# A four-layer conditional chain on one core: which engine casts x, and when the mixing matrices are made

## The reference

```
layers 0 and 2 (mix):  h   = gelu(gelu(cond @ W0 + b0) @ W1 + b1)
                       att = softmax(h @ W2 + b2)                  # 8 weights per example
                       out = (sum_k att[k] * weight[k]) @ x + att @ bias_k
layers 1 and 3 (conv): out = conv1d(x, weight, 9 taps, pad 4, 4 groups)
                             + cond @ c_weight.T + side
```

## Time and profile before

| | us |
|---|---|
| median of 3 runs | 2923.36 (2922.13 to 2923.71) |
| the profiled execution | 2924.14 |
| its span, first to last instruction | 2922.3 |
| TensorE busy | 2888.9 (99%) |
| VectorE busy | 2396.4 (82%) |
| ScalarE busy | 1394.9 (48%) |
| GpSimd busy | 1411.1 (48%) |
| mean granted TensorE clock | 0.992 of full |

### The profile page before, as it was taken

One profiled execution on the slowest core, in us unless ns is written; L12 is line 12 of the kernel. 1 busy time (PEld: TensorE's weight loads), 2 busy tenths in 40 slices (PEclk: granted clock), 3 DMA queues, 4 the chain that ended last, 5 costly groups with the idle time before them and its releaser, 6 DMA issues.

```text
span 2922.3 us, 123031 instructions
## 1 busy us (share of the span) xinstructions
PE 2888.9 (99%) x49220; PEld 2878.5 (99%) x49220; DVE 2396.4 (82%) x3099; ACT 1394.9 (48%) x2077; POOL 1411.1 (48%) x1545
## 2 busy tenths in 40 slices
PE   6999999999999999999999999999999999999998
PEld 5999999999999999999999999999999999999998
DVE  7888888878888887888888888878888888888884
ACT  3545454444445454544444454544444444545444
POOL 3454444545454444445454545445454545444442
PEclk7999999999999999999999999999999999999999
DMA  4777777777777777777777777777777777777774
GB/s 136 187 195 203 199 202 201 198 201 201 201 195 201 200 200 199 202 199 198 200 201 201 196 203 202 195 200 202 202 196 202 198 201 197 204 203 194 200 203 135
DMA packets 375112, 573.69 MB, mean 196 GB/s; under 512 B 63400, under 2 KB 227376, under 8 KB 358704
## 3 DMA queue, kind: packets, MB, share of 16 engines
q1 hardware_dynamic: 326320, 506.70, 64.8%
q10 hardware_dynamic: 48768, 66.65, 9.2%
HBM read 272.15 MB, written 167.77 MB: 151 GB/s over the span
## 4 chain that ended last, share of the span: by engine, by line
PE 97%; DVE 1%; DMA 1%; ACT 0%; ACTq 0%; SPq 0%; issue 0%; DVEq 0%
PE ps L309 73%; PE ps L294 24%; DMA x_t<-x 1%; ACT x_t L455 0%; DVE prod L528 0%; DVE xp L494 0%; DVE m_sum L532 0%; ACTq L471 0%; DVE m_own L536 0%; DVE y L563 0%; ACT y L430 0%; SPq L178 0%; DVE conv_raw L502 0%; DVE att_table L515 0%; DMA mixed<-m_own 0%
## 5 line engine op out<-in xcount | busy, mean ns | idle before, releaser
L309 PE MATMUL ps<-y,conv_parts 32*128 32x512 f32 x36864 | 2590.2, 390 | 2.2 <-DVE y L563 2.2
L309 PEld LDWEIGHTS ps<-y,conv_parts 32*128 32x128 f32 x36864 | 2469.9, 183 | 7.3 <-issue 3.3
L563 DVE SCALAR_TENSOR_TENSOR y<-ps,bias,y 128x512 fp32r<-128x512 f32 x1536 | 1066.9, 746 | 450.5 <-ACT y L430 443.8
L430 ACT ACTIVATE y<-ps,bias 128x512 fp32r<-128x512 f32 x1536 | 1047.0, 690 | 763.3 <-PE ps L309 718.0
L632 POOL TENSOR_TENSOR xp<-x_t,xp 128x512 fp32r<-128x512 f32 x512 | 709.9, 1417 | 564.3 <-DVE xp L494 564.3
L458 ACT ACTIVATE o_ph<-ps,bias 128x512 f32<-128x512 f32 x508 | 327.8, 687 | 736.4 <-PE ps L309 733.5
L639 POOL COPY o_t<-o_ch 128x512 f32<-128x512 f32 x508 | 636.0, 1373 | 9.7 <-DMA o_ch<-o_ph 9.7
L294 PE MATMUL ps<-y,m_parts 32*128 32x512 f32 x6144 | 582.2, 391 | 7.4 <-DVE y L563 7.4
L294 PE MATMUL ps<-xp,m_parts 32*128 32x512 f32 x6144 | 585.2, 391 | 0.8 <-issue 0.5
L626 POOL COPY bias<-bias_table 128x4 f32 (+3 forms) x512 | 94.8, 201 | 928.0 <-DMA o_ch<-o_ph 881.4
L294 PEld LDWEIGHTS ps<-y,m_parts 32*128 32x128 f32 x6144 | 524.9, 183 | 8.1 <-issue 7.8
(11 more groups left out here) (40 smaller groups left out, 43.4 us busy)
## 6 DMA issues: line engine op xcount, KB each, us to landing
x_t<-x SPq DMA_DIRECT2D x512, 256.0 KB, 5.3
m_parts<-mixed SPq DMA_DIRECT2D x1024, 128.0 KB, 5.2
out<-o_t SPq DMA_DIRECT2D x127, 1024.0 KB, 3.9
o_ch<-o_ph SPq DMA_DIRECT2D x1016, 64.0 KB, 2.0
o_ch<-o_ph ACTq DMA_DIRECT2D x1016, 64.0 KB, 2.1
mixed<-m_own SPq DMA_DIRECT2D x256, 128.0 KB, 2.4
conv_raw<-conv_w SPq DMA_DIRECT2D x2, 768.0 KB, 11.2
mix_sb<-mix_w SPq DMA_DIRECT2D x2, 576.0 KB, 11.2
```

What stands on the lines that cost most here:

```text
L309: ins = nc.tensor.matmul(ps[:, 4 + t, :], conv_parts[layer][rows, w, PH * q + p_in, :], src[rows, a, p_in, q:q + N], start=(k == 0), stop= ...
L430: nc.scalar.activation(dst, src, ACT.Identity, bias=bias[layer][:, k % WIDTH[layer]:k % WIDTH[layer] + 1]).then_inc(high_set[layer], 1)
L563: nc.vector.scalar_tensor_tensor(out=dst, in0=src, scalar=bias[layer][:, k % WIDTH[layer]:k % WIDTH[layer] + 1], in1=high.bitcast(fp32), o ...
```

## The change

VectorE's program before the steps puts `att_rows(0)` and matrix (0, 0) directly behind the softmax. `x_high` moves from VectorE to ScalarE: `x_high(0)` behind ScalarE's `att_rows(0)`, and in the steps behind the high parts of layer 0. The identity of conv 1 comes behind matrix (0, 0) and the `att_t` copies. Matrix (0, 1) is made ahead of the low part of conv 1's taps. The matrix of layer 2 is made one step later: matrix (2, i) in step i instead of matrix (2, i + 1). SP's transfers follow: x of example 1 is loaded in step -1 directly behind matrix (0, 0), and the store of matrix (2, i) stands behind the shuffle DMAs.

```diff
--- before.py
+++ after.py
@@ -215,18 +215,22 @@
                 if has(i, inner, 3):
                     sp.wait_ge(in_time_set, 4 * (i - 2))
                     sp.dma_start(out[i - 3], o_t[:]).then_inc(out_done, 16)
+                if not inner and i == -1:
+                    sp.wait_ge(x_low_set, 4)
+                    load_x(1)
+                if not inner and i == 0:
+                    store_matrix(2, 0)
+                    load_matrix(2, 0, True)
                 if has(i, inner, -2):
                     store_matrix(0, i + 2)
-                if has(i, inner, -1):
-                    store_matrix(2, i + 1)
-                if not inner and i == -1:
-                    load_matrix(2, 0, True)
                 if has(i, inner, 2) and (inner or not is_last(i)):
                     for g in range(G // 2):
                         sp.wait_ge(phases_set, nth(i - 2, g))
                         for p in range(PH):
                             sp.dma_start(o_ch[CG * g:CG * (g + 1), p, :], o_ph[CG * p:CG * (p + 1), g, :]).then_inc(shuffled[p], 16)
-                if has(i, inner, -2):
+                if has(i, inner, 0) and (inner or i != 0):
+                    store_matrix(2, i)
+                if has(i, inner, -2) and (inner or i != -1):
                     sp.wait_ge(x_low_set, 4 * (i + 2))
                     load_x(i + 2)
                 if not inner and is_last(i):
@@ -407,7 +411,16 @@
                 nc.scalar.copy(att_table[:, :, l, 0:4].rearrange("c j k -> c k j"),
                                ps[:, 6 - 2 * l, :].rearrange("c (k j) -> c k j", k=4)).then_inc(table_act, 1)
 
+            def x_high(j, first):
+
+                act.wait_ge(x_in, 16 * G * (j + 1))
+                if not first:
+                    act.wait_ge(mm[0], 4 * j)
+                for g in range(G):
+                    nc.scalar.copy(xp[:, HIGH, g, :], x_t[:, g, :]).then_inc(x_high_set, 1)
+
             att_rows(0)
+            x_high(0, True)
             conv_high_part(1)
             att_rows(1)
             for l in range(2):
@@ -438,6 +451,8 @@
                 if now:
                     for q in range(G):
                         high(0, i, q, segment(HIGH, q), by_phase(q), not inner and i == 0)
+                if now and has(i, inner, -1):
+                    x_high(i + 1, False)
                 if before:
                     final = not inner and is_last(i)
                     for g in range(G):
@@ -485,14 +500,6 @@
                 ins.then_inc(dve_chain, 1)
                 dve.wait_ge(dve_chain, chained[0])
 
-            def x_high(j, first):
-
-                dve.wait_ge(x_in, 16 * G * (j + 1))
-                if not first:
-                    dve.wait_ge(mm[0], 4 * j)
-                for g in range(G):
-                    nc.vector.tensor_copy(xp[:, HIGH, g, :], x_t[:, g, :]).then_inc(x_high_set, 1)
-
             def conv_identity(layer):
 
                 dve.wait_ge(conv_in[layer], 16)
@@ -548,15 +555,16 @@
                 dve.wait_ge(expo_set, l + 1)
                 chain(nc.vector.reciprocal(inv[:, l:l + 1], total[:, l:l + 1]))
                 nc.vector.tensor_scalar(att_sb[:, l, :], expo[:, l, :], inv[:, l:l + 1], None, ALU.mult).then_inc(att_set, 1)
-            x_high(0, True)
-            conv_identity(1)
             att_rows(0)
             matrix(0, 0, True)
             for l in range(2):
                 dve.wait_ge(att_t_mm, l + 1)
                 nc.vector.tensor_copy(att_t[:, l, :], ps[0:K, l, 0:B]).then_inc(att_t_set, 1)
+            conv_identity(1)
             att_rows(1)
+            matrix(0, 1, False)
             conv_low_part(1)
+
             def low(layer, j, k, dst, src, high):
 
                 dve.wait_ge(high_set[layer], nth(j, k))
@@ -572,13 +580,11 @@
                     for q in range(G):
                         low(0, i, q, segment(LOW, q), by_phase(q), segment(HIGH, q))
                 if not inner and i == 0:
-                    x_high(i + 1, False)
-                if has(i, inner, -2):
+                    matrix(2, 0, True)
+                if now and has(i, inner, -2):
                     matrix(0, i + 2, False)
-                if has(i, inner, -1):
-                    matrix(2, i + 1, not inner and i == -1)
-                if now and has(i, inner, -1) and (inner or i != 0):
-                    x_high(i + 1, False)
+                if now and (inner or i != 0):
+                    matrix(2, i, False)
                 if not inner and is_last(i):
                     dve.wait_ge(bias_set[3], B)
                     dve.wait_ge(x_low_set, 4 * B)
```

## The result

The changed kernel takes 2910.51 us (median of 6 runs, 2907.53 to 2912.03), the kernel before 2923.33 on the same chip (2922.13 to 2923.71): 12.8 us less, ratio 0.9955 [0.9945, 0.9966] (in brackets here and below: the 95% interval of the ratio). The sign and the mechanism came as written, but the forecast gain is 3.5 us too small. The profiled execution took 2910.93 with a span of 2908.7 (before 2922.3), at a mean clock of 0.995.

What follows compares the result with a forecast made beforehand. TensorE, 99% busy, was taken to bound the kernel, winnable only in its waits before the loop is full. Example 2 9.3 us earlier (9.0 + 2.2 - 1.9), loop 0: from 2923.36 to 2914.0 us, range 2910.8 to 2919.

Steps and rivals of the forecast that it cites:

- Which wait bounds the kernel: Before the loop is full: TensorE's 7.42 us wait ahead of layer 2 of example 0, on VectorE, delayed by late x.
- Part 1, matrix (0, 0): At the start: first matrix ends at 20.2, held by GpSimd (bounds 18.2 and 20.5), so layer 0 starts 2.0 us earlier.
- Part 2, the clock: From layer 0 of example 0 to example 1: of 2.0 us gained, 1.1 arrives, by when the clock rises; example 1 at 47.0.
- Part 3, layer 2: Layer 2 of example 0 starts at 52.1, not 61.11: 9.0 us gained, bounds 51 and 53.7.
- Part 3, the clock in the dip: From layer 2 of example 0 to example 2: the clock no longer falls, 2.2 us gained (bounds 0 and 2.2).
- Part 3, VectorE late at example 2: Layer 0 of example 2 waits for bank 0, freed late by VectorE: 1.9 us lost (bounds 0 and 3.7).
- Part 4, the loop: In the full loop: ScalarE's added casts and VectorE's held matrices stay covered, 0 change (bounds 0 and +0.3 a step).
- Rival C: In the loop: GpSimd holds VectorE until bank 0 comes late every step; slower, 2939; chance 0.07.
- B: Before example 2: the clock falls in the thin stretch, and VectorE or layer 2 is later; 2918; chance 0.13.
- D: At layer 2 of example 0: matrix (2, 0) or x of example 1 is late, start near 58; 2920.5; chance 0.07.
- E: At the start: matrices slip unheld between GpSimd's operations and the clock rises 3 us earlier; 12 us, 2911; chance 0.04.

Runs made afterwards that it cites:

- Experiment 1: Kernel before, with only the load of x for example 1 issued early, behind the first matrix load: 2915.66 us against 2923.11.
- experiment 2: Kernel before, with only the cast of x moved from VectorE to ScalarE: 2912.22 us, ratio 0.9963.
- 3: Kernel before, with only matrix (0, 0) directly behind the softmax, ahead of VectorE's cast of x and the identity: 2925.71 us, ratio 1.0009.
- 13: Kernel of 12, with GpSimd's low parts of x of example 0 waiting until matrix (0, 0) is done: 2911.62 us, ratio 0.9961.
- experiment 7: The changed kernel unedited, timed and profiled a second time: 2911.66 us, ratio 0.9962 to the kernel before.
- 4: Changed kernel, with the load of x for example 1 late again, behind the load of matrix (0, 1): 2910.55 us, ratio 0.9956 to the kernel before.
- 5: Changed kernel, with the cast of x back on VectorE, behind the matrices: 2913.30 us, ratio 0.9965 to the kernel before.
- 12: Changed kernel, with the added matmuls of 11 and conv 3's tap subtraction one step later on GpSimd: 2909.07 us, ratio 0.9956 to the kernel before.
- 8: Changed kernel, with GpSimd's subtraction for conv 3's taps one step later, ahead of x of example 2: 2913.56 us, ratio 0.997 to the kernel before.
- experiment 14: Kernel of 12, with VectorE's low parts of layer 2 ahead of matrix (2, 1) in step 1: 2910.83 us, ratio 0.9955 to the kernel before.
- 6: Changed kernel, with layer 2's matrix made one step earlier as before, and matrix (0, 1) and SP's stores in old order: 2910.93 us, ratio 0.9958.
- 11: Changed kernel, with twelve unused matmuls on TensorE: four ahead of the bias matmuls, two ahead of layer 0, six ahead of layer 1: 2909.33 us, ratio 0.9954.
- 9: Changed kernel, with VectorE's low parts of layer 2 ahead of matrix (2, 1) in step 1: 2912.65 us, ratio 0.9962 to the kernel before.
- experiment 10: Changed kernel, with four unused matmuls on TensorE ahead of the bias matmuls: 2909.26 us, ratio 0.9952 to the kernel before.

## Why the mechanism of the prediction was right, and which of its sizes failed

The mechanism was right and the sum too small: example 2 came 3.8 us ahead of its 65.2. Half of that is one mis-sized term, the late VectorE of part 3 (1.9 us charged, 0.0 measured); the next is the clock of part 2 (1.1 of 2.0 us carried on to example 1, where 2.5 of 2.7 were). Layer 2 started at 50.18, ahead even of that step's own early bound of 51.

- **Which wait bounds the kernel: right.** Layer 2 waited for VectorE's fifth low part, and VectorE for x. Experiment 1 removes the late load alone, and the wait goes from 7.42 to 1.76; experiment 2 takes the cast away, and it goes to nothing.
- **Part 1, matrix (0, 0): 2.7 us, not 2.0.** The contention was real and, as walked, near its size: 2.0 us of holds were forecast (matrix at 20.2, not 18.2), and product, cast and subtraction lost 0.08, 0.77 and 0.96, in all 1.8. But the rule of one whole GpSimd operation (1.35) for each did not come out. The rest is the product's start, 0.6 us ahead of its 14.8, with the weights there at 14.16 and not 14.73. In 3 and in 13 the matrix runs free and ends at 17.6 and 17.9, not 19.3, and layer 0 starts later all the same: what was moved out of its way came late instead. And most of this part is the cast's move, not the order: experiment 2, with the old order, has layer 0 at 25.48.
- **Part 2, the clock: this term failed, in its size.** I took 1.1 us between "the clock rises at the same moment" and "4.1 us behind the start of layer 1". It rose 4.4 us behind it, and 2.5 us arrived at example 1: 1.4 more than forecast, 0.7 of them from part 1. The term can't be had better than this from one profile each: experiment 7 and experiment 1 (layer 1 at 33.91, with the kernel before's order up to there) show that this moment differs between executions. x was no wait, as said (4: not even when loaded late).
- **Part 3, layer 2: 10.9 us, not 9.0.** 1.4 of the difference is what part 2 brought. The other 0.5 is layer 0 of example 1, which needs 4.61 us to layer 2, and not 5.1.
- **Part 3, the clock in the dip: right, 2.2.** 61.11 to 74.51 took 13.4 us, 50.18 to 61.41 takes 11.2.
- **Part 3, VectorE late at example 2: this term failed, in its size.** Minus 1.9 was forecast; the wait is 0.0, and 0.8 in experiment 7. The walk had GpSimd at x to 44.5 and its long subtraction to 48.2; they end at 41.3 and 45.9. The small cast is caught behind the subtraction as forecast (43.93 to 45.97), but 2 us earlier, so the low parts begin at 46.49 and not 48.5. And matrices (0, 3) and (2, 1) run from 51.92 to 60.32 with 1.8 us of holds, where the walk had 3.2 and an end at 64.4: the x of example 2 reaches GpSimd at 55.48, when the first of them is done. Bank 0 is thus free near 61.0, and TensorE is ready at 61.41. In experiment 7 the x is there at 54.41, both matrices are held, and the wait is 0.8. Experiments 5 (1.25), 12 (1.0) and 8 (2.60) have this wait too. With it the sum closes: 1.4 + 0.5 + 1.9 = 3.8 us.
- **Part 4, the loop: right.** ScalarE's cast takes 617 ns, between the bounds of 0.49 and 0.69; VectorE is held by 1.8 us a matrix, and the step stays at 22.30. Rival C had the holding right, but not the limit: of the 4 us of spare that were walked 3 are left. The span behind example 2 is 0.5 us shorter, where I had 0: one wait of TensorE near the end, 0.54 us, is gone; no experiment looked into why.
- **The rivals.** B (the clock falls in the thin stretch) is false for the changed kernel; experiment 12 shows such a fall once, experiment 14, with the same matmuls up to there, does not. B's reason, that layer 0's thin work holds the clock at half, is not borne out: in experiments 1, 3, 6 and 11 to 14 this work ran at full clock. D's own wait, for matrix (2, 0), came in no version; the same kind of wait, for matrix (2, 1) at layer 2 of example 1, is 1.00 us in 1, 1.06 in 5 and 2.62 in 9. E has the number (2911), but not for its reasons: the matrices were held, and the clock rose 2.4 us earlier than before (39.5, not 41.9), no more than the 2.7 us by which layer 1 started earlier. That its edge and the median agree within 0.3 us is luck.

What stays open: why the clock falls behind the thin stretch in experiment 12 and not in 14 or in the changed kernel; and what sets the moment at which it rises in layer 0 or layer 1.

## What to carry to other kernels

When one queue is late for a transfer, moving the transfer and taking the waiting work off the queue are two cures for one wait: cost them together, and don't add their gains (7.5 and 10.9 alone, 12.8 with both and the first matrix). A short operation behind a long one decides who starts next: in experiment 3 a 0.47 us copy cost the 4.6 us gained ahead of it. And of a gain at the start ask where the next queue has slack: here 5.5 us more at example 1 (12) and 4.9 at example 2 (14) ended as 2.6 us and as no gain that can be told. And before reading terms of 1 us from milestones, profile the unchanged program twice (7).

## What the runs showed of the hardware

- VectorE and GpSimd hold each other, and at the start the ends fit whole operations: a 128-column cast of 0.23 us, begun at 43.93, ended at 45.97, GpSimd's long subtraction at 45.88; in experiment 1 it took 3.29. The same four 32-column adds took 0.47 us with GpSimd idle and 3.73 beside its subtractions (13). In the loop a cast begun at 1007.96 took 2.42 us beside GpSimd copies of 1.3 each, so a hold can outlast one operation. The reduction took 1.35 us in all cases.
- In the first 30 us the granted clock fell in a wait of TensorE: at 19 in the changed kernel (a wait of 4.61 us), at 25.5 in experiment 10 (2.78), at 24.6 in 13 (2.63). In 11, 12 and 14, with no recorded wait above 0.82 us between 15 and 44, it was 1.00 from 15 to 46, and layer 0 to layer 1 took 6.6 us; in the versions without added matmuls it took 6.7 to 9.9.
- Once the clock fell with no wait recorded for TensorE since 32 us: to 0.52 over 46.5 to 50 in 12, behind a stretch with some strips idle. The same thin work in 14 and in the changed kernel left it up.
- ScalarE's cast of 512 columns takes 617 ns, VectorE's 0.9 beside GpSimd (3.63 for four): 2.5 us a step for ScalarE. VectorE lost 3.6 us of cast a step and is held for 3.7 more on its two matrices; its busy time rose from 2396.4 to 2410.9 us.
